# Scores of a cross attention from high and low parts in f32r, with the keys' low part made by the vector engine

## The chip, the cores and the metric

One core of one Trainium2 chip. The metric is the device time of one execution in microseconds. The kernel is one program that computes two decoder layers; the change is in its first stage.

## The reference, cut to what matters

The stage is the cross attention of layer 0. 8 sequences of 64 query tokens (512 wide, 16 heads of 32) look at a context of 1601 tokens of width 256. The last 16 tokens are handled apart; the main attention is over 1585 keys.

```python
q = _ln((x @ Wq + bq).reshape(b, s1, H, HD), qn_w, qn_b)
kv = jnp.concatenate([y_main @ Wk + bk, y_main @ Wv + bv], axis=-1)
kv = kv.reshape(b, s2, H, 2 * HD)
k = _ln(kv[..., :HD], kn_w, kn_b)
v = kv[..., HD:]
s = jnp.einsum('bhqd,bhkd->bhqk', q, k) * SCALE
p = jax.nn.softmax(s, axis=-1)
ctx = jnp.einsum('bhqk,bhkd->bhqd', p, v)
```

## The kernel before

`x0_main_attention` goes through the sequences one at a time, in two halves of 8 heads each. A half has 13 key tiles of 128 keys (the last has 49), so a sequence is 26 tile steps, numbered n = 0 to 25. All engines run the same list of steps, each its own part in a fixed order, tied by semaphores; between the first and the last sequence a hardware loop does two sequences a turn.

In step n:
- PE writes the scores of tile n, for 8 heads and 64 queries at once, into one of two PSUM banks (L828): two matmuls, g = 0 and 1, of 128 keys by 256 columns, with the keys `kT` as weights and `qbd` as moving operand. `qbd` holds the queries of four heads on a block diagonal, zero elsewhere, so that one matmul does four heads. PE waits for `kept` of tile n-2 first.
- DVE first subtracts the maximum from tile n-14 (L961), then scales tile n by the keys' inverse deviations while it moves it to the ring in SBUF (L983, `kept`), then takes the running maximum (L993).
- ACT does the exponential of tile n-14 (L1078), POOL adds it to the running sum (L889), and PE multiplies tile n-16 with the values (L854).
- At n = 14 and n = 1 a half's maximum is finished: PE transposes the running maximum (L838, one step earlier), DVE reduces it and rounds it (L1000, L1002, L1004), and PE spreads it (L799). `L799` stands ahead of all other work of PE in its step and waits for L1004.

Between these stand entries of four kinds, placed at steps by two strings: Y (transpose of the context), K (projection of keys), W (sums of squares of the keys, for the deviations) and V (projection of values). `HERE` are those for the sequence at hand, `AHEAD` those for the next:

```python
HERE = entries("0:K030 1:K031 2:W03 3:K100 4:K101 4:V0 5:W10 5:V1 6:K110 6:V2 7:K111 7:V3 8:W11 8:V4 9:K120 9:V5 "
               "10:K121 10:V6 11:W12 11:V7 12:V8 13:K130 13:V9 14:K131 14:Va 15:W13 15:Vb 16:Vc")
AHEAD = entries("12:Y00 13:Y01 15:Y10 16:Y11 16:K000 17:K001 18:W00 18:Y20 19:K010 20:K011 21:W01 21:Y21 "
                "22:K020 23:K021 24:W02 24:Y30 25:Y31")
```

Each entry uses one of three PSUM banks in turn. PE fills it, and another engine reads it and frees it. For Y, ACT writes the high part of the transposed context in f32r (L1034) and DVE the low part, what is left of the exact value (L111 by `split`). For K, ACT writes the keys with their bias to `kT` in f32 (L1040) and their squares to `sq` (L1042), and frees the bank. The projections Y feeds are already done with three f32r matmuls each, high by high, high by low and low by high (`matmul3`, L116 to L118).

DVE places the queries of the half after next in `qbd` at n = 0 and n = 13 (`place_queries`, four instructions of 32 rows, L913).

Of the kernel before, what the change touches and what calls it, by code (L numbers as in the profile page):

```python
# [14 lines left out]
F32 = mybir.dt.float32  # L15
F32R = mybir.dt.float32r
# [282 lines left out]
def half_at(part, n, step):  # L299

    for f in (-2, -1, 0, 1):
        if n == KT * f + step and not (f < 0 and part == "first"):
            return f
    return None
# [324 lines left out]
def x0_main_attention(nc, c, d, ps, qT, wkv, bk, kn, ctxT, y, load_context, y_loaded):  # L629
# [5 lines left out]
    with Stage(nc, "x0b") as st:  # L635
# [6 lines left out]
        kT = st.sb("kT", [P, 2, MAIN0])  # L642
# [3 lines left out]
        qbd = st.sb("qbd", [P, HG0, GC])  # L646
# [37 lines left out]
        for part, batches in (("prologue", [("before", -1), ("first", 0)]), ("body", [("body", 0), ("body", 1)]),  # L684
# [3 lines left out]
            for kind, rel in batches:  # L688
                for e in (BEFORE if kind == "before" else [(a, *e) for n in range(TILES) for a, e in made_at(kind, n)]):
# [7 lines left out]
                                                      st.sem("w_done"), st.sem("rstd_done"))  # L697
        v_done, q_placed = st.sem("v_done"), st.sem("q_placed")
# [24 lines left out]
        def place(at, e):  # L723
            part, i, rel = at
            return sched.find(part, i, (rel, *e))

        with nc.Block() as block:
# [9 lines left out]
            def _(pe):  # L737
# [54 lines left out]
                def step(part, at, seq, par, n):  # L792
# [25 lines left out]
                    if n < TILES:  # L818
# [8 lines left out]
                        for g in range(2):  # L827
                            mm = pe.matmul(ps[0:m, S_BANK + n % 2, g * GC:(g + 1) * GC], kT[:, g, kt * P:kt * P + m],  # L828
                                           qbd[:, 2 * half + g, :], start=True, stop=True)
# [67 lines left out]
            def _(v):  # L897
                v.memset(qbd[:, :, :], 0.0).then_inc(zeroed, 1)
# [3 lines left out]
                v.wait_ge(zeroed, 4)  # L902
                for j in range(4):
                    v.memset(headsum[32 * j:32 * j + 32, j:j + 1], 1.0).then_inc(zeroed, 1)
                v.wait_ge(zeroed, 8)
# [4 lines left out]
                def place_queries(seq, half):  # L910
                    for j in range(4):
                        rows = slice(32 * j, 32 * j + 32)
                        v.tensor_scalar(qbd[rows, 2 * half:2 * half + 2, S * j:S * j + S],  # L913
                                        qT[rows, 2 * half:2 * half + 2, bass.ds(seq * S, S)], kn[rows, 0:1], None, ALU.mult
                                        ).then_inc(q_placed, 1)

                def take(at, seq, e):
                    bank, nth = place(at, e)
                    if e[1] == "Y":
# [105 lines left out]
            def _(act):  # L1025
                def take(at, seq, e):
# [8 lines left out]
                    if e[1] == "K":  # L1035
# [4 lines left out]
                        act.activation(kT[:, g, k0:k0 + n], src[:, 0:n], ACT.Identity, bias=bias).then_inc(k_done, 1)  # L1040
                        act.wait_ge(w_made, 8 * seq + (4 * half + j + 1))
                        act.activation(sq[g][:, 0:n], src[:, 0:n], ACT.Square, bias=bias).then_inc(sq_done, 1)  # L1042
                        act.wait_ge(sq_done, 16 * seq + (8 * half + 2 * j + g + 1))
                        act.sem_inc(kv_free[bank], 1)
# [20 lines left out]

                def step(part, at, seq, par, n):
                    f = half_at(part, n, 29)
# [2045 lines left out]
```

## Time and profile before

| | us |
|---|---|
| median of 3 runs | 2758.72 (2758.25 to 2759.28) |
| the profiled execution, its own time | 2750.2 |
| its span in the profile | 2747.5 |
| PE busy in the span | 2434.7 (89%) |
| DVE busy | 1719.2 (63%) |
| ACT busy | 1155.4 (42%) |
| POOL busy | 1002.0 (36%) |

The span goes from the first to the last instruction of the profiled execution. Busy time of PE is that of matmul records, whose ends are modelled; weight loads are recorded apart (PEld). An f32 matmul appears as two records. "Granted clock" is TensorE's clock as a share of 2.4 GHz. The first cross attention's main part begins at about 103 us and ends at about 973 us.

### The profile page before, as it was taken

The numbers are of one execution on the slowest core, as the hardware profiler recorded it, in microseconds if no ns is written. First come the engines' busy times: TensorE is split into PE (matmuls) and PEld (weight loads), VectorE is DVE, ScalarE is ACT, GpSimd is POOL, SyncE is SP. The second block draws the span as 40 slices with busy tenths as digits, with TensorE's granted clock in tenths as the row PEclk, the third lists the DMA queues.
The fourth block names the chain that finished last, engine by engine and source line by source line (L and its number), as shares of the span: only waits on it lengthen the run. The fifth ranks groups of instructions, "written<-read, shape, count | busy, mean of one in ns | idle before, by whom it ended". The sixth has DMA issues, their size and how long they took to land. (4 is left out here: it accounts for less than half of the span.)

```text
span 2747.5 us, 40047 instructions
## 1 busy us (share of the span) xinstructions
PE 2434.7 (89%) x12756; PEld 2003.8 (73%) x12756; DVE 1719.2 (63%) x2728; ACT 1155.4 (42%) x2084; POOL 1002.0 (36%) x688
## 2 busy tenths in 40 slices
PE   4699999999999969998898899999999997788744
PEld 2588888888888748886676678888888876566632
DVE  3457766766767723333443278888788884666677
ACT  1344444443444313332221367666676662332211
POOL 3147667667667610000011035544555460110000
PEclk9699999999999979998899899999999999899957
DMA  3000000000000012210231200000000002110010
GB/s 103 1 25 25 25 1 25 25 1 25 19 7 1 1 64 69 68 61 17 68 86 37 83 25 25 16 18 17 26 25 16 10 1 76 52 41 31 12 62 16
DMA packets 104256, 89.51 MB, mean 33 GB/s; under 512 B 32752, under 2 KB 82432, under 8 KB 104080
## 3 DMA queue, kind: packets, MB, share of 16 engines
q1 hardware_dynamic: 103792, 87.28, 10.5%
q8 instruction: 96, 1.57, 0.2%
q14 instruction: 80, 0.66, 0.1%
q0 software_dynamic: 288, 0.00, 0.0%
HBM read 86.22 MB, written 1.05 MB: 32 GB/s over the span
## 5 line engine op out<-in xcount | busy, mean ns | idle before, releaser
L2184 POOL TENSOR_TENSOR xT<-xT,x1b_ring 128x512 f32<-128x512 f32 (+1 forms) x176 | 248.3, 1411 | 213.4 <-ACT x1b_ring L2314 206.7
L869 POOL TENSOR_TENSOR x0b_krstd<-x0b_krstd,minus_half 128x24 f32<-128x24 f32 x64 | 267.0, 4173 | 108.7 <-DVE x0b_krstd L933 87.9
L889 POOL TENSOR_TENSOR xT<-xT,x0b_ring 128x512 f32<-128x512 f32 (+1 forms) x176 | 243.8, 1385 | 142.4 <-ACT x0b_ring L1078 130.6
L983 DVE TENSOR_TENSOR x0b_ring<-x_ps,x0b_krstd 128x512 f32<-128x512 f32 (+1 forms) x208 | 143.0, 688 | 134.4 <-PE x_ps L828 132.2
L111 DVE TENSOR_TENSOR x1b_plo<-x1b_ring,x1b_phi 128x512 fp32r<-128x512 f32 (+1 forms) x208 | 222.2, 1068 | 6.6 <-issue 4.9
L854 PE MATMUL x_ps<-x0b_ring,x0b_vn 128*128 128x256 f32 (+1 forms) x832 | 217.5, 386 | 1.8 <-ACT x0b_ring L1078 1.6
L828 PE MATMUL x_ps<-x0b_qbd,x0b_kT 128*128 128x256 f32 (+1 forms) x832 | 217.6, 384 | 1.6 <-DVE x0b_ring L983 1.4
L1078 ACT ACTIVATE x0b_ring<-x0b_ring 128x512 f32<-128x512 f32 (+1 forms) x208 | 130.7, 630 | 207.7 <-DVE x0b_ring L961 197.3
L2329 ACT ACTIVATE x1b_ring<-x_ps,x1b_keymask 128x512 f32<-128x512 f32 (+1 forms) x208 | 143.1, 688 | 131.3 <-DVE xT L2256 126.0
L116 PE MATMUL x_ps<-x1b_qy,x1b_yT 128*128 128x512 f32 (+1 forms) x416 | 175.8, 423 | 4.3 <-ACT x1b_ring L2329 2.9
L828 PEld LDWEIGHTS x_ps<-x0b_qbd,x0b_kT 128*128 128x128 f32 (+1 forms) x832 | 149.9, 187 | 30.1 <-issue 6.4
L854 PEld LDWEIGHTS x_ps<-x0b_ring,x0b_vn 128*128 128x128 f32 (+1 forms) x832 | 153.4, 191 | 23.9 <-issue 2.7
L116 PE MATMUL x_ps<-x1b_phi,x1b_yv 128*128 128x512 f32 (+1 forms) x416 | 166.6, 400 | 1.5 <-ACT x1b_out_sb L2296 1.5
L2256 DVE SCALAR_TENSOR_TENSOR xT<-x_ps,x1b_keymask,xT 128x512 f32<-128x512 f32 (+1 forms) x176 | 131.2, 745 | 57.7 <-PE x_ps L118 56.8
L993 DVE TENSOR_TENSOR xT<-xT,x0b_ring 128x512 f32<-128x512 f32 (+1 forms) x176 | 153.5, 872 | 17.9
L117 PE MATMUL x_ps<-x1b_qy,x1b_yT 128*128 128x512 f32 (+1 forms) x416 | 164.4, 395 | 0.0
L118 PE MATMUL x_ps<-x1b_qy,x1b_yT 128*128 128x512 f32 (+1 forms) x416 | 164.4, 395 | 0.0
L118 PE MATMUL x_ps<-x1b_phi,x1b_yv 128*128 128x512 f32 (+1 forms) x416 | 163.9, 394 | 0.0
L117 PE MATMUL x_ps<-x1b_plo,x1b_yv 128*128 128x512 f32 (+1 forms) x416 | 163.2, 392 | 0.0
L2314 ACT ACTIVATE x1b_ring<-x1b_ring 128x512 f32<-128x512 f32 (+1 forms) x208 | 131.1, 630 | 64.0 <-DVE x1b_ring L2225 63.0
L961 DVE TENSOR_TENSOR x0b_ring<-x0b_ring,x_ps 128x512 f32<-128x512 f32 (+1 forms) x208 | 141.3, 683 | 24.7 <-PE x_ps L799 10.6
L2225 DVE TENSOR_TENSOR x1b_ring<-x1b_ring,x_ps 128x512 f32<-128x512 f32 (+1 forms) x208 | 140.6, 676 | 2.0 <-PE x_ps L2094 2.0
(575 smaller groups left out, 5844.5 us busy)
## 6 DMA issues: line engine op xcount, KB each, us to landing
x_y<-in_ctx_dram SPq DMA_DIRECT2D x8, 1536.0 KB
x_y<-in_ctx_dram SPq DMA_DIRECT2D x24, 512.0 KB, 3.8
a_wn<-in_L_attn_W_Q_dram SPq DMA_DIRECT2D x16, 256.0 KB, 3.1
a_wn<-in_L_attn_W_K_dram SPq DMA_DIRECT2D x16, 256.0 KB, 3.5
a_wn<-in_L_attn_W_V_dram SPq DMA_DIRECT2D x16, 256.0 KB, 4.1
a_won<-in_L_attn_W_O_dram SPq DMA_DIRECT2D x16, 256.0 KB, 2.9
x1a_wq<-in_L_xattn_Wq_dram SPq DMA_DIRECT2D x4, 1024.0 KB, 10.7
x1c_wo<-in_L_xattn_Wo_dram SPq DMA_DIRECT2D x8, 512.0 KB, 6.9
```

Source lines behind the costliest of these rows:

```text
L111: return v.tensor_tensor(lo, exact, hi.bitcast(F32), ALU.subtract)
L116: pe.matmul(out, lhs[0], rhs[0], start=start, stop=False, **kw)
L117: pe.matmul(out, lhs[0], rhs[1], start=False, stop=False, **kw)
L118: return pe.matmul(out, lhs[1], rhs[0], start=False, stop=stop, **kw)
L828: mm = pe.matmul(ps[0:m, S_BANK + n % 2, g * GC:(g + 1) * GC], kT[:, g, kt * P:kt * P + m], qbd[:, 2 * half + g, :], start=True, stop=True)
L854: mm = pe.matmul(ps[:, O_BANK, g * GC:(g + 1) * GC], vn[0:m, kt, half, g * P:(g + 1) * P], ring[0:m, key_slot(par, t, LIFE), g * GC:(g + 1 ...
L869: ins = g_.tensor_tensor(r, r, c.minus_half[:, 0:8].unsqueeze(1).broadcast_to([P, whole, 8]), ALU.pow)
L889: g_.tensor_tensor(total[half][0:m, :], old, src, ALU.add).then_inc(summed, 1)
L983: v.tensor_tensor(slot.rearrange("p (h s) -> p h s", s=S), ps[0:m, S_BANK + n % 2, :].rearrange("p (h s) -> p h s", s=S), spread(krstd[0:m ...
L993: v.tensor_tensor(run[half][0:m, :], before, slot, ALU.max).then_inc(max_done, 1)
L2184: g_.tensor_tensor(total[half][0:m, :], old, src, ALU.add).then_inc(summed, 1)
L2329: act.activation(ring[0:m, key_slot(par, n, LIFE), :], ps[0:m, S_BANK + n % 2, :], ACT.Identity, bias=keymask[0:m, kt:kt + 1]).then_inc(ke ...
```

## The change

`kT` and `qbd` become pairs of f32r tiles, a high and a low part. The scores are taken with `matmul3`. For each K entry ACT squares first, then writes the high part of the keys; DVE reads the same bank again, adds the bias, subtracts the high part and writes the low part, and then frees the bank. For the queries ACT writes the high part into the block diagonal and DVE the low part, each in four instructions of 32 rows. Both `qbd` tiles are zeroed at the start.

```diff
-        kT = st.sb("kT", [P, 2, MAIN0])
+        kT = [st.sb(f"kT{i}", [P, 2, MAIN0], F32R) for i in ("hi", "lo")]
-        qbd = st.sb("qbd", [P, HG0, GC])
+        qbd = [st.sb(f"qbd{i}", [P, HG0, GC], F32R) for i in ("hi", "lo")]
...
                         for g in range(2):
-                            mm = pe.matmul(ps[0:m, S_BANK + n % 2, g * GC:(g + 1) * GC], kT[:, g, kt * P:kt * P + m],
-                                           qbd[:, 2 * half + g, :], start=True, stop=True)
+                            mm = matmul3(pe, ps[0:m, S_BANK + n % 2, g * GC:(g + 1) * GC],
+                                         [a[:, g, kt * P:kt * P + m] for a in kT], [a[:, 2 * half + g, :] for a in qbd],
+                                         start=True, stop=True)
...
             def _(v):
-                v.memset(qbd[:, :, :], 0.0).then_inc(zeroed, 1)
+                for a in qbd:
+                    v.memset(a[:, :, :].bitcast(F32), 0.0).then_inc(zeroed, 1)
...
-                        v.tensor_scalar(qbd[rows, 2 * half:2 * half + 2, S * j:S * j + S],
-                                        qT[rows, 2 * half:2 * half + 2, bass.ds(seq * S, S)], kn[rows, 0:1], None, ALU.mult
-                                        ).then_inc(q_placed, 1)
+                        hi, lo = (a[rows, 2 * half:2 * half + 2, S * j:S * j + S] for a in qbd)
+                        v.wait_ge(q_hi, 8 * seq + (4 * half + j + 1))
+                        v.scalar_tensor_tensor(lo, qT[rows, 2 * half:2 * half + 2, bass.ds(seq * S, S)], kn[rows, 0:1],
+                                               hi.bitcast(F32), ALU.mult, ALU.subtract).then_inc(q_placed, 1)
...
+                    if e[1] == "K":
+                        _, _, half, j, g = e
+                        k0, n = keys_of(j)
+                        i = 16 * seq + (8 * half + 2 * j + g + 1)
+                        hi, lo = (a[:, g, k0:k0 + n] for a in kT)
+                        v.wait_ge(k_hi, i)
+                        v.scalar_tensor_tensor(lo, ps[:, bank, 0:n], kbias[:, 2 * half + g:2 * half + g + 1],
+                                               hi.bitcast(F32), ALU.add, ALU.subtract).then_inc(k_done, 1)
+                        v.wait_ge(k_done, i)
+                        v.sem_inc(kv_free[bank], 1)
...
                         act.wait_ge(kv_full[bank], nth + 1)
-                        act.activation(kT[:, g, k0:k0 + n], src[:, 0:n], ACT.Identity, bias=bias).then_inc(k_done, 1)
                         act.wait_ge(w_made, 8 * seq + (4 * half + j + 1))
                         act.activation(sq[g][:, 0:n], src[:, 0:n], ACT.Square, bias=bias).then_inc(sq_done, 1)
-                        act.wait_ge(sq_done, 16 * seq + (8 * half + 2 * j + g + 1))
-                        act.sem_inc(kv_free[bank], 1)
+                        act.activation(kT[0][:, g, k0:k0 + n], src[:, 0:n], ACT.Identity, bias=bias).then_inc(k_hi, 1)
...
+                def place_queries(seq, half):
+                    for j in range(4):
+                        rows = slice(32 * j, 32 * j + 32)
+                        act.activation(qbd[0][rows, 2 * half:2 * half + 2, S * j:S * j + S],
+                                       qT[rows, 2 * half:2 * half + 2, bass.ds(seq * S, S)], ACT.Copy, scale=kn[rows, 0:1]
+                                       ).then_inc(q_hi, 1)
+
+                act.wait_ge(zeroed, 9)
+                place_queries(0, 0)
+
                 def step(part, at, seq, par, n):
+                    if n == 0:
+                        if part != "first":
+                            act.wait_ge(scored, TILES * seq)
+                        place_queries(seq, 1)
+                    if n == KT and part != "last":
+                        act.wait_ge(scored, TILES * seq + KT)
+                        place_queries(seq + 1, 0)
```

## Rows read from the trace of the kernel before

**Rows 1.** Windows: span, busy us of each engine (instructions), granted clock, DMA share, GB/s.

```profile
185.00:972.00 787.00, 753.71 (x4026) 649.49 (x4025) 544.34 (x919) 340.34 (x601) 523.61 (x264) 0.99 0.04 13
497.21:544.57 47.36, 45.90 (x256) 39.73 (x257) 37.01 (x64) 21.90 (x41) 33.69 (x17) 1.00 0.06 16
544.57:599.26 54.69, 54.12 (x288) 47.08 (x289) 34.96 (x58) 23.71 (x41) 35.24 (x18) 1.00 0.05 17
```

**Rows 2.** Waits, 199 to 972 us: who for whom, us, times, longest.

```profile
DVE x0b_ring L983 <- PE x_ps L828: 111.5, 88, 3.1
...
DVE x0b_yT L111 <- ACT x0b_yT L1034: 37.4, 29, 2.7
...
PE x_ps L799 <- DVE x0b_rowmax L1004: 20.9, 13, 5.4
```

**Rows 3.** Timeline of PE, two places: start, us, line, operation, count.

```profile
207.58 0.34 PE L117 MATMUL x_ps<-x0b_yT,x_wkv 128*128 128x384 f32 x1
...
208.28 0.34 PE L118 MATMUL x_ps<-x0b_yT,x_wkv 128*128 128x384 f32 x1
...
519.33 1.03 PE L828 MATMUL x_ps<-x0b_qbd,x0b_kT 128*128 128x256 f32 x4
...
522.11 1.03 PE L828 MATMUL x_ps<-x0b_qbd,x0b_kT 128*128 128x256 f32 x4
```

**Rows 4.** One line's instructions: duration in ns, least, median, most.

```profile
L828 PE MATMUL x_ps<-x0b_qbd,x0b_kT x832: 377/379/634, 141.0 to 940.4; 128*128 128x256 f32 x154, 128*49 128x256 f32 x13
```

**Rows 5.** Timeline of PE in a later stage, f32 of 128 columns.

```profile
1022.57 3.74 PE L1274 MATMUL a_ps<-a_wvT,xT 128*128 128x128 f32 x32
```

**Rows 6.** Timeline of DVE in the light stretch.

```profile
513.76 0.69 DVE L961 TENSOR_TENSOR x0b_ring<-x0b_ring,x_ps 128x512 f32<-128x512 f32 x1 [0.15 <-DVE x0b_yT L111]
...
523.36 0.68 DVE L961 TENSOR_TENSOR x0b_ring<-x0b_ring,x_ps 128x512 f32<-128x512 f32 x1
...
525.37 0.68 DVE L961 TENSOR_TENSOR x0b_ring<-x0b_ring,x_ps 128x512 f32<-128x512 f32 x1
...
528.36 0.69 DVE L111 TENSOR_TENSOR x0b_yT<-x_ps,x0b_yT 128x512 fp32r<-128x512 f32 x1 [0.80 <-ACT x0b_yT L1034]
...
532.24 0.69 DVE L983 TENSOR_TENSOR x0b_ring<-x_ps,x0b_krstd 128x512 f32<-128x512 f32 x1 [0.33 <-PE x_ps L828]
...
535.02 0.69 DVE L983 TENSOR_TENSOR x0b_ring<-x_ps,x0b_krstd 128x512 f32<-128x512 f32 x1 [0.68 <-PE x_ps L828]
...
537.91 0.21 DVE L111 TENSOR_TENSOR x0b_yT<-x_ps,x0b_yT 128x49 fp32r<-128x49 f32 x1 [0.24 <-DVE x0b_krstd L933]
...
540.82 1.21 DVE L913 TENSOR_SCALAR x0b_qbd<-x_qT,x_kn 32x128 f32 x4 [0.34 <-PE x_ps L828]
...
544.28 0.16 DVE L1004 TENSOR_TENSOR x0b_rowmax<-x0b_rowmax,x0b_qshift 128x4 f32<-128x4 f32 x1
```

**Rows 7.** Timeline of PE: three of L799, with the idle time before.

```profile
440.08 1.11 PE L799 MATMUL x_ps<-ident,x0b_rowmax 128*128 128x128 f32 x4 [5.21 <-DVE x0b_rowmax L1004]
...
497.21 0.65 PE L799 MATMUL x_ps<-ident,x0b_rowmax 128*128 128x128 f32 x4 [0.21 <-DVE x0b_rowmax L1004]
...
544.57 0.65 PE L799 MATMUL x_ps<-ident,x0b_rowmax 128*128 128x128 f32 x4 [1.46 <-DVE x0b_rowmax L1004]
```

**Rows 8.** Timeline of ACT in one step of the same stretch.

```profile
524.07 0.63 ACT L1078 ACTIVATE x0b_ring<-x0b_ring 128x512 f32<-128x512 f32 x1 [0.44 <-DVE x0b_ring L961]
524.61 0.57 ACT L1040 ACTIVATE x0b_kT<-x_ps,x0b_kbias 128x384 f32<-128x384 f32 x1
525.07 0.57 ACT L1042 ACTIVATE x0b_sq<-x_ps,x0b_kbias 128x384 f32<-128x384 f32 x1
```

**Rows 9.** A scalar_tensor_tensor from PSUM in a later stage, duration in ns.

```profile
L2256 DVE SCALAR_TENSOR_TENSOR xT<-x_ps,x1b_keymask,xT x176: 733/747/753, 1585.8 to 2238.2; 128x512 f32<-128x512 f32 x160, 65x512 f32<-65x512 f32 x16
```

**Rows 10.** Timeline at the start of the main part.

```profile
103.33 0.91 DVE L898 MEMSET x0b_qbd<- 128x1024 f32 x1 [5.15 <-PEq L383]
```

**Rows 11.** Windows, behind the wait at 440.08.

```profile
440.00:444.00 4.00, 3.92 (x12) 3.47 (x13) 1.71 (x3) 0.63 (x1) 0.00 (x0) 0.50 0.00 0
```

More of the change, by code:

```diff
@@ L697, in x0_main_attention @@
                                                       st.sem("w_done"), st.sem("rstd_done"))
+        k_hi, q_hi = st.sem("k_hi"), st.sem("q_hi")
         v_done, q_placed = st.sem("v_done"), st.sem("q_placed")
@@ L901, in _ @@
                     v.memset(a[:, :, MAIN0:MAIN0 + 1].bitcast(F32), 0.0).then_inc(zeroed, 1)
-                v.wait_ge(zeroed, 4)
+                v.wait_ge(zeroed, 5)
                 for j in range(4):
                     v.memset(headsum[32 * j:32 * j + 32, j:j + 1], 1.0).then_inc(zeroed, 1)
-                v.wait_ge(zeroed, 8)
+                v.wait_ge(zeroed, 9)
                 v.tensor_scalar(headkn[:, :], headsum[:, :], kn[:, 1:2], None, ALU.mult).then_inc(ready, 1)
```

## The prediction

> **What bounds the kernel now.** I read the windows first. The first cross attention's main part runs from 185 to 972 us. There TensorE (PE) is busy 753.7 of 787.0 us at full clock, VectorE (DVE) 544.3, ScalarE (ACT) 340.3 and GpSimd (POOL) 523.6 [rows 1]. So PE sets the pace on average. But the same view, cut at the places where PE stands still (below), shows two unlike halves of one batch. From tile step 1 to 14 (54.69 us) DVE is busy 35.0 us. From step 14 to step 1 of the next batch (47.36 us) it is busy 37.0 us [rows 1]. The schedule strings explain it: value projections stand only at steps 4 to 16, so PE's long steps are there, and steps 17 to 25 hold little more than scores, probabilities-times-values and a key projection.
>
> The waits say the same from the other side [rows 2]. DVE stands 111.5 us for the scores of PE, which is slack. PE stands 20.9 us for the row maxima of L1004, which is the place where DVE sets the end: L799 at steps 14 and 1 waits for it, and all later PE work is behind L799. So a batch is two stretches, each ended by that wait. I call 1 to 14 the heavy stretch and 14 to 1 the light one.
>
> **Price of the scores.** A 256-column f32 matmul is two records. Four records of L828 span 1.03 us and one record lasts 379 ns, so records start (1.03-0.38)/3 = 0.217 us apart, 0.868 us a tile [rows 3, 4]. The new form issues six f32r matmuls of 256 columns a tile. The trace has none of that size. Its nearest is 384 columns: five starts over 0.70 us, 0.175 apart, which is 0.160 of streaming (384 columns at 2.4 GHz, the granted clock being 1.00) and 0.015 more [rows 1, 3]. At 256 columns that makes 0.107+0.015 = 0.122, and a tile 0.732 us. I take this. Lower bound: pure streaming, 0.107, a tile 0.64. Upper bound: a weight load that no longer hides; 32 records of a 128x128 load with 0.107 us of streaming in f32 take 3.74 us, at most 0.117 each [rows 5], so loads do keep up at that pace, and the bound from far off is the 0.175 of the 384-column form, a tile 1.05 us.
>
> The Trainium skill ("TensorE: Matmul & The Clock Gate", Part 3, The mechanism) speaks against the change: it says a weight load overlaps a running matmul only when the row groups differ. With its load of columns/1.2 ns a record would be about 0.107+0.107 us, and the tile 1.28 us against 0.87, an estimate of +86 us over 208 tiles. The 384-column records, 0.175 apart with a 128-column load in each, do not agree with it; by it they would be 0.27 apart.
>
> So PE is relieved of 0.868-0.732 = 0.136 us a tile, 28.3 us over 208 tiles (bounds: 47 us less, 38 us more). What arrives at the end depends on who paces.
>
> **Heavy stretch, PE paces.** DVE has some 20 us of idle time there [rows 1] and takes its share of the new work within it: half a batch's 16 K entries, at most 8 x 0.8 = 6 us. Steps 1 to 13 give 13 x 0.136 = 1.77 us. The wait at step 14 was 0.21 us [rows 7]; its chain (score of tile 12, placing of queries, tile 13, row maximum) does not shorten with the score of tile 13 and gets about 0.1 us longer, since the first ACT copy must precede DVE's first subtraction. I take 1.5 us a batch, 8 batches: -12 us.
>
> **Light stretch, DVE paces.** From its subtraction at step 17 (513.76) to the end of the row maximum (544.28 + 0.16) DVE works 30.7 us, and its waits for others are only 0.80 (L111), 0.33 and 0.68 (L983) and 0.34 (L913): 2.15 us [rows 6]. Its bare step is 25.37-23.36 = 2.01 us. PE's step with a key projection is 522.11-519.33 = 2.78 us, 2.64 after the change [rows 3].
> - New DVE instruction: one scalar_tensor_tensor from PSUM for each of 16 K entries a batch. At 128x512 that operation takes 0.747 us [rows 9]; the tensor_tensor L111 takes 0.69 at 512 and 0.21 at 49 elements, so 1.04 ns an element [rows 6]. For 384 elements: 0.61 us (bounds 0.56 in proportion, 0.75 as it stands). Behind it DVE waits for its own write before it frees the bank, 0.15 us as after L111 [rows 6]: 0.76 us.
> - New wait: DVE now stands for ACT's high part, as it did for L111. ACT's order is exponential, square, high part. In a saturated step DVE's subtraction starts at 523.36, ACT's exponential at 524.07, its two K operations at 524.61 and 525.07, and the second ends 525.64 [rows 8], 2.28 us after the subtraction. DVE is free after 2.01. So each handover costs about 0.27 us even with PE ahead. The step is 2.28+0.76 = 3.04 us, more than PE's 2.64: PE then runs at most two tiles ahead (it waits for `kept` of tile n-2) and stands still. Behind DVE's wait stand the next subtraction and so ACT's next exponential; the K bank is freed later too, but with three banks its next user comes two steps later.
> - Six K entries lie in the saturated part (steps 16, 17, 19, 20, 22, 23). Six instructions: 4.56 us. Four handovers (at 16 and 17 ACT is early): 1.08. Together 5.64. The idle 2.15 us vanishes into them. Placing adds 0.1. PE reaches step 17 earlier by 3 x 0.136 = 0.4. Net 5.64-2.15+0.1-0.4 = +3.2 us for each of the seven light stretches that hold a next batch: +22 us. If no handover cost anything it would be +2.1 each, +15; if each of the six took 0.75+0.15 and waited 0.3, +4.7, +33. The last batch has no K entries there: nothing.
>
> **The rest.** Eight 32-row query copies a batch go to ACT, which is idle over half the time [rows 1], each shorter than the 0.46 us between two K operations [rows 8], while DVE still finishes its last split. Without that cover 16 times four of them would be at most 29 us. The first placing is not covered: four copies stand ahead of ACT's first output, and a second memset of 0.91 us [rows 10] ahead of the first matmul, together +2.5 us. Squares now come first, so the four W entries before batch 0 start one ACT operation earlier, 4 x 0.46 = 1.8 less. Net +1 (bounds -1 to +3). The keys' high part costs ACT what the plain copy cost. No DMA changes.
>
> **Sum.** -12+22+1 = +11 us. The profiled execution took 2750.2 us (span 2747.5) and the median of the runs is 2758.7, 8.5 more, so 2761 in the profile and **2770 us** in the median.
>
> **Rivals.**
> 1. *PE paces everywhere (the other side).* The 111.5 us for which DVE waits [rows 2] hides all its new work, and all 28.3 us arrive: 2758.7-28.3+1 = 2731 us. It decides where a light K step of DVE stays under PE's 2.64 us, against the 3.04 worked out. Against it: that slack is in the heavy stretch. With the 0.107 records it would reach 2713. Chance 0.18.
> 2. *The handover is as long as L111's.* There DVE waited 37.4 us for ACT in 29 waits, 1.3 us each, or 0.8 over the 48 large ones of 8 batches [rows 2]. Six waits of 0.8 a stretch instead of 1.08 in all: +3.7x7 = 26, 2796 us. Against it: the long ones are at Y entries whose transposes come last in PE's step. Chance 0.13.
> 3. *Loads show at 256 columns.* A record takes 0.145, nothing is gained on PE: +12 heavy, +3 light, 2785 us. By the skill's rule above it would be far worse. Chance 0.07.
> 4. *The clock.* At 440.08 PE stood 5.21 us, and over the next 4 us the granted clock was 0.50, that is 1.2 GHz [rows 7, 11]; after the 1.46 us at 544.57 it stayed 1.00. The following heavy stretch is 57.1 against 54.7 us. If the longer stand at step 1 does this in five more light stretches: up to 5 x 2.4, taken as +9, 2779 us. The skill's same page (HAM oscillation) also warns of it. For it: PE's stand before L838 and L799 grows by over 3 us. Against it: part is spread over the scores. Chance 0.15.
>
> **Numbers.** The forecast has chance 0.47, and its own range is 2758 to 2784. From 2738 to 2798 about half of rival 1 and half of rival 2 fall outside, 0.15 in all. Measurement tells 0.2%, 5.5 us. Faster is rival 1 and a sliver of the main case, 0.20; within 0.2% is the low tail of the main case, 0.12; slower is the rest, 0.68.
>
> **What would show it.** Records of L116 to L118 with kT and qbd 0.12 us apart (under 0.11 or over 0.14 is wrong). Heavy stretches (L799 to L799) near 53 us, light ones near 50.5 or more with PE idle before L828, L838 and L799. New DVE instructions near 0.61 us, their waits for ACT about 0.3 in the light stretch. DVE waits for L828 nearly gone from steps 17 to 25. The prediction is wrong if light stretches get shorter, which means DVE was not the pacer; or if heavy ones grow, which means banks held longer stop PE, a cost put at nothing here.

## The result and the profile after

The changed kernel takes 2791.01 us (median of 4 runs, 2789.17 to 2794.21), the kernel before 2758.48 beside it (4 runs). The ratio is 1.0135, with a 95% interval of 1.0116 to 1.0155: slower by 33 us by the medians and by 37 by the ratio, where +11 was forecast. I call it 35 below. The profiled execution of the changed kernel took 2789.17 us and its span is 2787.4, against 2747.5 before. One execution each of e6_low_later and e14_spread_no_low below fell in a slower state of the chip and is left out of their times and run counts.

Lines have moved: old L799 is L800 (its last operand from DVE, old L1004, is now L1018), L838 is L840, L828 is now L116 to L118, L961 is L975, L983 is L997, L993 is L1007. L929 is the new instruction for the keys' low part, L932 frees its bank, L918 is the queries' low part, L1055 ACT's square, L1056 its high part of the keys, L1081 that of the queries, L770 PE's sums of squares. L1107 is ACT's exponential, L856 PE's product with the values; L1014 and L1016 are the first two instructions of the row maximum (old L1000 and L1002); L1023 and L1030 add a finished half to the context.

I cut both traces at L799/L800 into seven pairs of stretches and added them up:

| stretches | before | after | difference | forecast |
|---|---|---|---|---|
| seven light ones (step 14 to step 1) | 337.6 | 371.6 | +34.0, 4.9 each | +3.2 each |
| seven heavy ones (step 1 to step 14) | 384.6 | 392.5 | +7.9, 1.1 each | -1.5 each |

So both halves missed to the same side. All else together is 2 us shorter. Windows of the changed kernel: us, busy us of PE, PEld, DVE, ACT and POOL (instructions), granted clock, DMA share, GB/s. The rows of before are [rows 1].

```profile
185.00:980.00 795.00, 729.32 (x4317) 653.61 (x4316) 608.95 (x999) 343.27 (x635) 505.72 (x248) 0.95 0.04 13
566.12:622.32 56.20, 53.53 (x314) 48.01 (x314) 43.11 (x67) 24.89 (x46) 34.09 (x17) 0.97 0.03 9
512.79:566.12 53.33, 47.36 (x283) 42.73 (x283) 41.59 (x73) 22.93 (x44) 35.62 (x17) 0.94 0.08 23
346.00:348.00 2.00, 2.00 (x7) 1.77 (x7) 1.16 (x2) 0.73 (x2) 0.00 (x0) 0.50 0.00 0
540.00:544.00 4.00, 1.44 (x13) 1.24 (x11) 3.54 (x5) 1.72 (x4) 3.75 (x3) 0.97 0.00 0
544.00:548.00 4.00, 4.00 (x16) 3.64 (x16) 3.35 (x7) 1.14 (x2) 2.92 (x3) 0.50 0.00 0
566.00:570.00 4.00, 3.88 (x26) 3.68 (x27) 2.74 (x5) 1.77 (x3) 0.00 (x0) 1.00 0.38 121
582.00:586.00 4.00, 2.01 (x9) 1.59 (x9) 3.59 (x7) 0.63 (x1) 1.18 (x1) 0.84 0.00 0
586.00:590.00 4.00, 4.00 (x19) 3.52 (x18) 2.08 (x4) 1.23 (x2) 3.97 (x2) 0.73 0.00 0
```

The third row is a light stretch (before 47.36 us), the second the heavy one behind it (before 54.69). In the light one PE is idle for 6 us where it was idle for 1.5. The granted clock of the whole part fell from 0.99 to 0.95, and the small windows show where: it is 0.50 (1.2 GHz) right behind one stand of PE (540 to 544), and the 0.84 and 0.73 around another are means of both levels. Behind the stand at step 1 it stays 1.00 in this batch (566 to 570), but not in every one: two batches earlier (346 to 348) it is 0.50. Of the seven heavy stretches four lose the full clock behind step 1 and four behind step 5.

What PE waited for, 199 to 1010 us, and two of DVE's waits (us, times, longest):

```profile
DVE x0b_kTlo L929 <- ACT x0b_kThi L1056: 41.7, 63, 1.9
DVE x0b_ring L997 <- PE x_ps L118: 34.3, 54, 2.6
PE x_ps L800 <- DVE x0b_rowmax L1018: 29.5, 14, 5.4
...
PE x_ps L770 <- ACT x0b_sq L1055: 16.1, 8, 2.6
...
PE x_ps L116 <- DVEq L932: 12.1, 7, 2.0
...
PE x_ps L840 <- DVE xT L1007: 6.0, 6, 2.8
```

DVE's slack against PE's scores went from 111.5 to 34.3 us [rows 2]. PE's wait for the row maximum grew from 20.9 to 29.5, and two waits are large that were not in [rows 2]: for the squares (L770) and for a bank that DVE has not freed (L932). PE around these places:

```profile
344.38 0.65 PE L800 MATMUL x_ps<-ident,x0b_rowmax 128*128 128x128 f32 x4 [2.82 <-DVE x0b_rowmax L1018]
...
539.88 0.27 PE L117 MATMUL x_ps<-x0b_qbdlo,x0b_kThi 128*128 128x256 f32 x1
540.00 0.28 PE L118 MATMUL x_ps<-x0b_qbdhi,x0b_kTlo 128*128 128x256 f32 x1
542.83 1.88 PE L770 MATMUL x_ps<-x0b_headsum,x0b_sq 128*128 128x4 f32 x12 [2.56 <-ACT x0b_sq L1055]
...
545.46 1.91 PE L856 MATMUL x_ps<-x0b_ring,x0b_vn 128*128 128x256 f32 x4
...
566.12 0.65 PE L800 MATMUL x_ps<-ident,x0b_rowmax 128*128 128x128 f32 x4 [2.83 <-DVE x0b_rowmax L1018]
...
576.51 0.28 PE L118 MATMUL x_ps<-x0b_qbdhi,x0b_kTlo 128*128 128x256 f32 x1
576.63 0.28 PE L116 MATMUL x_ps<-x0b_qbdhi,x0b_kThi 128*128 128x256 f32 x1
576.76 0.27 PE L117 MATMUL x_ps<-x0b_qbdlo,x0b_kThi 128*128 128x256 f32 x1
...
581.00 1.40 PE L770 MATMUL x_ps<-x0b_headsum,x0b_sq 128*128 128x4 f32 x12
584.39 0.50 PE L116 MATMUL x_ps<-x_wkv,x0b_yT 128*128 128x512 f32 x1 [1.99 <-DVEq L932]
```

The score records start 0.12 us apart (539.88 to 540.00, 576.51 to 576.63), as forecast. DVE at the same places:

```profile
537.86 0.69 DVE L975 TENSOR_TENSOR x0b_ring<-x0b_ring,x_ps 128x512 f32<-128x512 f32 x1 [0.15 <-DVE x0b_yT L111]
...
540.19 0.62 DVE L929 SCALAR_TENSOR_TENSOR x0b_kTlo<-x_ps,x0b_kbias,x0b_kThi 128x384 fp32r<-128x384 f32 x1 [0.22 <-ACT x0b_kThi L1056]
540.96 0.69 DVE L975 TENSOR_TENSOR x0b_ring<-x0b_ring,x_ps 128x512 f32<-128x512 f32 x1 [0.15 <-DVE x0b_kTlo L929]
...
551.78 0.62 DVE L929 SCALAR_TENSOR_TENSOR x0b_kTlo<-x_ps,x0b_kbias,x0b_kThi 128x384 fp32r<-128x384 f32 x1 [1.58 <-ACT x0b_kThi L1056]
...
561.05 1.47 DVE L918 SCALAR_TENSOR_TENSOR x0b_qbdlo<-x_qT,x_kn,x0b_qbdhi 32x128 fp32r<-32x128 f32 x4 [0.41 <-ACT x0b_qbdhi L1081]
...
564.58 1.21 DVE L1016 TENSOR_TENSOR x0b_rowmax<-x0b_rowmax,x0b_qshift 128x4 f32<-128x4 f32 x1
...
580.40 0.67 DVE L1023 TENSOR_TENSOR x0b_osb<-x0b_osb,x_ps 128x512 f32<-128x512 f32 x1
581.21 2.42 DVE L1030 TENSOR_TENSOR x_ctxT<-x0b_osb,x_ctxT 32x128 f32 x4
583.66 0.62 DVE L929 SCALAR_TENSOR_TENSOR x0b_kTlo<-x_ps,x0b_kbias,x0b_kThi 128x384 fp32r<-128x384 f32 x1
```

And ACT before the stand at 540:

```profile
541.68 0.63 ACT L1107 ACTIVATE x0b_ring<-x0b_ring 128x512 f32<-128x512 f32 x1 [1.53 <-DVE x0b_ring L975]
542.22 0.56 ACT L1055 ACTIVATE x0b_sq<-x_ps,x0b_kbias 128x384 f32<-128x384 f32 x1
```

Three readings.
- **Step 21 (540 us).** DVE's step with a K entry is 3.10 us (L975 at 537.86 and 540.96; forecast 3.04). DVE falls behind PE, its subtraction comes late, ACT's exponential waits for it, ACT's square stands behind the exponential, and PE's sums of squares (W01) wait for the square: 2.56 us. The same stand of 2.56 us is there in the six light stretches from 291 on. The forecast had only the scores, L838 and L799 in mind as the places where DVE's lateness reaches PE.
- **Step 5 (584 us).** DVE's low part of a K entry stands behind the accumulation of the finished half: one L1023 and four L1030, 3.2 us from 580.40. The bank is held as long, and PE's next projection into it (V1) stands 1.99 us. Seven batches show this, with 1.25 to 2.00 us.
- **Step 1 (566 us).** The stand is 2.83 us where it was 1.46 [rows 7]. It is not the K entry that grew here: the queries' low parts take 1.47 instead of 1.21 us [rows 6] and L1016 takes 1.21 us, where the trace of before has 0.16 for it (old L1002) in the same place. Over all seven stands at step 1 the growth is smaller, 18.6 to 24.0 us, 0.8 each: it is 1.4 in three batches and not there at the turns of the hardware loop, where PE stood over 5 us already.

The traces also show what goes with a long L1016. Rows of before, DVE and POOL, and of the changed kernel, POOL:

```profile
544.08 0.16 DVE L1002 TENSOR_TENSOR x0b_rowmax<-x0b_rowmax,x0b_qshift 128x4 f32<-128x4 f32 x1
...
544.34 1.26 POOL L889 TENSOR_TENSOR xT<-xT,x0b_ring 49x512 f32<-49x512 f32 x1 [0.27 <-POOL xT L889]
...
564.51 1.25 POOL L891 TENSOR_TENSOR xT<-xT,x0b_ring 49x512 f32<-49x512 f32 x1 [0.27 <-POOL xT L891]
```

In the changed kernel POOL's instruction starts at 564.51, ahead of L1016 (564.58), and L1016 ends at 565.79, 0.03 us behind it. Before, POOL's starts at 544.34, when L1002 is done. All 14 long L1016 of the changed kernel and all 11 long L1002 of before have an instruction of POOL running at their start and end 0.02 to 0.04 us behind its end. No run moves POOL's work alone, so this is read and not tested.

The new instruction's price is as forecast. Groups by line and shape, 199 to 1010 us (busy us, mean ns of one, and the idle time before):

```profile
L929 DVE SCALAR_TENSOR_TENSOR x0b_kTlo<-x_ps,x0b_kbias,x0b_kThi 128x384 fp32r<-128x384 f32 x84 | 51.7, 616 | 29.2 <-ACT x0b_kThi L1056 28.4
...
L929 DVE SCALAR_TENSOR_TENSOR x0b_kTlo<-x_ps,x0b_kbias,x0b_kThi 128x433 fp32r<-128x433 f32 x28 | 18.7, 669 | 13.4 <-ACT x0b_kThi L1056 13.4
```

### The profile page after: what moved, and what is told of

The parts are those of the page before. It is cut to its first block and busy times, and to the rows that moved or that the text cites. A ratio compares the mean times of both kernels' runs of the same rounds, so it can differ in the third digit from the quotient of the medians.

```text
span 2787.4 us, 41223 instructions
## 1 busy us (share of the span) xinstructions
PE 2428.8 (87%) x13172; PEld 2023.7 (73%) x13172; DVE 1814.9 (65%) x2857; ACT 1172.7 (42%) x2148; POOL 1005.9 (36%) x688
## 3 DMA queue, kind: packets, MB, share of 16 engines
HBM read 86.22 MB, written 1.05 MB: 31 GB/s over the span
## 5 line engine op out<-in xcount | busy, mean ns | idle before, releaser
L1107 ACT ACTIVATE x0b_ring<-x0b_ring 128x512 f32<-128x512 f32 (+1 forms) x208 | 130.9, 631 | 309.9 <-DVE x0b_ring L975 308.7
L856 PE MATMUL x_ps<-x0b_ring,x0b_vn 128*128 128x256 f32 (+1 forms) x832 | 227.2, 399 | 1.9 <-ACT x0b_ring L1107 1.6
L116 PE MATMUL x_ps<-x1b_qy,x1b_yT 128*128 128x512 f32 (+1 forms) x416 | 176.0, 423 | 4.3 <-ACT x1b_ring L2358 2.9
L856 PEld LDWEIGHTS x_ps<-x0b_ring,x0b_vn 128*128 128x128 f32 (+1 forms) x832 | 159.6, 199 | 25.9 <-issue 3.2
L1007 DVE TENSOR_TENSOR xT<-xT,x0b_ring 128x512 f32<-128x512 f32 (+1 forms) x176 | 159.5, 906 | 19.0 <-DVE x0b_ring L997 1.5
L997 DVE TENSOR_TENSOR x0b_ring<-x_ps,x0b_krstd 128x512 f32<-128x512 f32 (+1 forms) x208 | 142.7, 686 | 44.0 <-PE x_ps L118 41.7
L116 PE MATMUL x_ps<-x1b_phi,x1b_yv 128*128 128x512 f32 (+1 forms) x416 | 166.3, 400 | 1.5 <-ACT x1b_out_sb L2325 1.5
L975 DVE TENSOR_TENSOR x0b_ring<-x0b_ring,x_ps 128x512 f32<-128x512 f32 (+1 forms) x208 | 142.0, 686 | 35.2 <-DVE x0b_kTlo L929 17.2
L118 PE MATMUL x_ps<-x1b_qy,x1b_yT 128*128 128x512 f32 (+1 forms) x416 | 164.3, 395 | 0.0
L118 PE MATMUL x_ps<-x1b_phi,x1b_yv 128*128 128x512 f32 (+1 forms) x416 | 164.1, 395 | 0.0
L116 PE MATMUL x_ps<-x0b_qbdhi,x0b_kThi 128*128 128x256 f32 (+1 forms) x416 | 152.2, 366 | 4.0 <-DVE x0b_ring L997 3.8
L111 POOL TENSOR_TENSOR x1b_yv<-x_y,x1b_yv 128x256 fp32r<-128x256 f32 (+1 forms) x104 | 87.2, 838 | 144.1 <-ACT x1b_yv L2372 142.8
```

What stands on the lines that cost most here:

```text
L111: return v.tensor_tensor(lo, exact, hi.bitcast(F32), ALU.subtract)
L116: pe.matmul(out, lhs[0], rhs[0], start=start, stop=False, **kw)
L118: return pe.matmul(out, lhs[1], rhs[0], start=False, stop=stop, **kw)
L856: mm = pe.matmul(ps[:, O_BANK, g * GC:(g + 1) * GC], vn[0:m, kt, half, g * P:(g + 1) * P], ring[0:m, key_slot(par, t, LIFE), g * GC:(g + 1 ...
L975: v.tensor_tensor(slot, slot, ps[0:m, M_BANK, :], ALU.subtract).then_inc(shifted, 1)
L997: v.tensor_tensor(slot.rearrange("p (h s) -> p h s", s=S), ps[0:m, S_BANK + n % 2, :].rearrange("p (h s) -> p h s", s=S), spread(krstd[0:m ...
```

## The experiments

My theory after the result: DVE's K work costs far more than its own time in stretches that it paces, because it also delays what others take from DVE in the heavy half. The rivals: the longer hold of the bank or the handover alone; the loss of the clock alone; PE's new score records giving nothing. All ratios are to the kernel before, run beside; one per cent is about 27.5 us. Sums are over the seven light and the seven heavy stretches of the profiled execution. That is one run and can lie off the median: by 10 us in e5 and 13 in e10, most of it behind this stage, by 8 (below) in the kernel before, by under 5 in the others.

**e1_no_low.** The low part of the keys is never made (POOL zeroes that tile once, and PE waits for it at the start); ACT frees the bank. The third matmul of each score still runs.

```diff
-                        v.wait_ge(k_hi, i)
-                        v.scalar_tensor_tensor(lo, ps[:, bank, 0:n], kbias[:, 2 * half + g:2 * half + g + 1],
-                                               hi.bitcast(F32), ALU.add, ALU.subtract).then_inc(k_done, 1)
-                        v.wait_ge(k_done, i)
-                        v.sem_inc(kv_free[bank], 1)
+                        pass
...
+                        act.wait_ge(k_done, 16 * seq + (8 * half + 2 * j + g + 1))
+                        act.sem_inc(kv_free[bank], 1)
```

> Leaves out the low part of the keys (that tile stays zero, so the third f32r matmul of each score adds nothing but still runs); ACT frees the K bank itself behind its two reads, as before the change. Theory A, the vector engine's new K instruction with its handover is the whole loss: the relief of PE arrives in full. Six records of 256 columns lie 0.118 us apart in the trace after, 0.71 us a tile instead of 0.868, so 208 x 0.158 = 33 us less than before and about 3 us more at the start: near 2729 us. Theory B, something else of the change loses the time (queries placed by two engines, the added waits of ACT): at or above 2758 us, and the light stretches stay over 50 us. Between them: each share as the time says.

Measured: 2735.97 us (4 runs), ratio 0.9933 [0.9918, 0.9947]. Light 336.6, heavy 374.7. Against the changed kernel that is 0.0202, some 56 us: the whole price of the K work on DVE. And without it the new scores gain only 18 us, not 28: the light stretches are as long as before (336.6 to 337.6). One part of that is the stand at step 1, which is 2.85 us here too and 5.9 us longer than before over the seven batches; the rest is not split up.

```profile
537.92 0.65 PE L802 MATMUL x_ps<-ident,x0b_rowmax 128*128 128x128 f32 x4 [2.85 <-DVE x0b_rowmax L1018]
```

Its DVE shows the same chain as the changed kernel's, queries' low parts and a long L1016, with no K work of DVE near.

```profile
533.34 1.10 DVE L922 SCALAR_TENSOR_TENSOR x0b_qbdlo<-x_qT,x_kn,x0b_qbdhi 32x128 fp32r<-32x128 f32 x3 [0.15 <-issue]
...
536.50 1.10 DVE L1016 TENSOR_TENSOR x0b_rowmax<-x0b_rowmax,x0b_qshift 128x4 f32<-128x4 f32 x1
```

**e2_hold_only.** DVE waits for ACT's high part and frees the bank, but makes no low part.

```diff
-                        v.scalar_tensor_tensor(lo, ps[:, bank, 0:n], kbias[:, 2 * half + g:2 * half + g + 1],
-                                               hi.bitcast(F32), ALU.add, ALU.subtract).then_inc(k_done, 1)
-                        v.wait_ge(k_done, i)
+                        v.sem_inc(k_done, 1)
```

> Leaves out the low part of the keys (that tile stays zero), but the vector engine still waits for ACT's high part in its place, and still is the one that frees the bank. If the instruction's own time on the vector engine (16 x 0.77 us a batch) is what costs: close to the kernel without any of it, within 8 us of 2729. If the handover and the bank held by the vector engine's late turn are what costs: close to the changed kernel, 2775 to 2790, with TensorE still standing 2 us for the bank at step 5 of each batch and for the squares at step 21.

Measured: 2747.33 us (10 runs), ratio 0.998 [0.9967, 0.9994]. Light 345.0, heavy 377.5. So the wait for ACT and the longer hold cost 0.0047 (13 us), and the instruction itself, with its own wait behind it, 0.0155 (43 us): from e2 to the changed kernel the light stretches grow by 26.6, 3.8 each, the heavy ones by 15.0, 2.1 each. The stand at step 5 is not there in e2: the bank's place in DVE's order alone does not make it. A heavy stretch of e2 has the same granted clock as that of the changed kernel, 0.97, with the half clock behind step 1; so what the low part costs there is mostly the stand at step 5 itself and not the clock behind it.

```profile
230.44:284.50 54.06, 53.38 (x315) 48.04 (x315) 35.10 (x58) 25.03 (x45) 34.28 (x17) 0.97 0.02 6
```

**e3_f32_scores.** All is made as in the changed kernel, but the score is one f32 matmul of the two high parts.

```diff
-                            mm = matmul3(pe, ps[0:m, S_BANK + n % 2, g * GC:(g + 1) * GC],
-                                         [a[:, g, kt * P:kt * P + m] for a in kT], [a[:, 2 * half + g, :] for a in qbd],
-                                         start=True, stop=True)
+                            mm = pe.matmul(ps[0:m, S_BANK + n % 2, g * GC:(g + 1) * GC],
+                                           kT[0][:, g, kt * P:kt * P + m].bitcast(F32),
+                                           qbd[0][:, 2 * half + g, :].bitcast(F32), start=True, stop=True)
```

> All of the change's work on ACT and DVE is kept, but the scores are again one f32 matmul each, of the high parts alone (the low parts are written and not read). It tells what f32r scores are worth once the vector engine has its new work. If DVE sets the pace in the light stretches and PE in the heavy ones: about half of 33 us is lost, 2791 + 12 to 20 = 2803 to 2811. If PE sets the pace everywhere: 2824. If DVE does everywhere: 2791 to 2795.

Measured: 2806.89 us (4 runs), ratio 1.019 [1.0175, 1.0205]. Light 367.6, heavy 408.8. The faster scores are worth 0.0055, 15 us, beside this DVE work; all of it is in the heavy stretches (408.8 to 392.5), and none in the light ones, which are 4 us longer with the faster scores (367.6 to 371.6). This is the plainest sign that DVE paces the light stretches.

**e6_low_later.** DVE takes a K entry one step later, behind that step's subtraction, so that ACT's high part is there already.

```diff
+                    while late:
+                        take(*late.pop(0))
...
-                        take(at, seq + ahead, (ahead, *e))
+                        if e[0] == "K":
+                            late.append((at, seq + ahead, (ahead, *e)))
+                        else:
+                            take(at, seq + ahead, (ahead, *e))
```

> Only the place of the vector engine's K work changes: it is taken one step later, behind that step's first subtraction. The subtraction then no longer waits for ACT's high part, and ACT's exponential and squares are released earlier; the bank is held some 0.8 us longer. If the handover loop (subtraction, exponential, square, high part, low part) and the squares that come late for PE are a large part of the loss: a light K step falls from 3.1 to about 2.8 us, the 2.6 us wait of PE for squares at step 21 shrinks, and the time falls to 2770 to 2780. If the bank held longer is what costs: 2795 or more, with PE's wait for a bank at step 5 longer than 2.0 us. If it is the instruction's time alone: 2788 to 2792.

Measured: 2804.62 us (5 runs), ratio 1.0186 [1.0172, 1.0199]. Light 387.0, heavy 393.7: 14 us worse than the change as it was made, all of it in the light stretches. PE's waits:

```profile
PE x_ps L116 <- DVEq L932: 19.3, 13, 1.8
...
PE x_ps L770 <- ACT x0b_sq L1061: 9.4, 7, 1.5
PE x_ps L116 <- DVE x0b_yT L111: 8.4, 6, 2.1
```

Sparing DVE its wait for ACT and holding the bank a step longer trades one for the other: the squares come earlier (16.1 to 9.4 us), but the stands for a bank go from 7 to 13 (12.1 to 19.3 us), and waits for the transposed context grow from 1.2 to 8.4. The wait for ACT was not the costly part, as e2 says too.

**e8_fill.** The changed kernel with work that PE does for nothing while it stands: 14 transposes of the identity before V1's wait for its bank (step 5), 20 before W01's wait for the squares (step 21).

```diff
+                def fill(read, count):
+                    pe.wait_ge(normed, read)
+                    for _ in range(count):
+                        pe.transpose(ps[:, X_BANK, 0:P], c.ident[:, :], c.ident[:, :])
+
...
+                    if e[1:] == ("V", 1):
+                        fill(2 * seq + 1, 14)
                     pe.wait_ge(kv_free[bank], nth + 1)
+                    if e[1:] == ("W", 0, 1) and at != ("prologue", 0, -1):
+                        fill(2 * seq, 20)
```

> The changed kernel with PE kept busy in two of its new stands: 14 transposes of the identity (0.11 us each) into an unused bank ahead of the wait for a bank at step 5, and 20 ahead of the wait for squares at step 21. The result is unchanged. If the half clock that follows those stands is a good part of the loss (granted clock 0.94 in light and 0.97 in heavy stretches against 1.00), PE keeps 2.4 GHz there, the light stretches fall by 1 us or more and the heavy ones by 1: 2770 to 2780. If the clock only slows PE where it waits for DVE anyway, nothing changes or it gets slower by what the transposes overrun: 2789 to 2800.

Measured: 2780.92 us (6 runs), ratio 1.0089 [1.0071, 1.0106]. Light 364.3, heavy 389.7. The granted clock from 199 to 900 us is 0.98, against 0.95 in the changed kernel and 0.99 before. PE is as late as it was, but busy:

```profile
539.27 2.35 PE L742 MATMUL x_ps<-ident 128*128 128x128 f32 x20
...
541.99 1.50 PE L779 MATMUL x_ps<-x0b_headsum,x0b_sq 128*128 128x4 f32 x12 [0.37 <-ACT x0b_sq L1064]
```

So about 13 us (0.0046) of the loss is time at half clock behind these stands. The rest, 0.0089, is there at nearly full clock: light stretches still 26.7 us over those of before, heavy ones 5.1. The half clock is not all gone: with the other two stands filled it lies behind the stand at step 1 in each of the seven heavy stretches. In the batch at 564:

```profile
565.00:569.00 4.00, 4.00 (x16) 3.50 (x15) 2.04 (x4) 1.77 (x3) 0.00 (x0) 0.57 0.02 6
```

**e4_spread, e5_spread_before, e14_spread_no_low.** The same strings of entries in three kernels: the changed one, the one before, and e1. Value projections are moved out of steps 5 to 15 until six of the 13 stand at steps 16 to 22 (one before), where PE had slack and DVE had none; three of the Y entries stand two steps later.

```diff
-        HERE = entries("0:K030 1:K031 2:W03 3:K100 4:K101 4:V0 5:W10 5:V1 6:K110 6:V2 7:K111 7:V3 8:W11 8:V4 9:K120 9:V5 "
-                       "10:K121 10:V6 11:W12 11:V7 12:V8 13:K130 13:V9 14:K131 14:Va 15:W13 15:Vb 16:Vc")
-        AHEAD = entries("12:Y00 13:Y01 15:Y10 16:Y11 16:K000 17:K001 18:W00 18:Y20 19:K010 20:K011 21:W01 21:Y21 "
+        HERE = entries("0:K030 1:K031 2:W03 3:K100 4:K101 4:V0 5:W10 6:K110 6:V1 7:K111 8:W11 8:V2 9:K120 10:K121 10:V3 "
+                       "11:W12 12:V4 13:K130 13:V5 14:K131 14:V6 15:W13 16:V7 17:V8 18:V9 19:Va 19:Vb 22:Vc")
+        AHEAD = entries("12:Y00 13:Y01 16:K000 17:Y10 17:K001 18:W00 18:Y11 19:K010 20:Y20 20:K011 21:W01 21:Y21 "
```

> The changed kernel with the schedule strings changed: the 13 value projections stand at steps 4 to 22 instead of 4 to 16, and the context transposes Y10, Y11 and Y20 two steps later, since the projections read the tiles that they overwrite. The same instructions in all. If DVE sets the pace in the light stretches and PE in the heavy ones, then moving PE work from the one to the other makes both engines' loads lie over each other: PE's total is about 96 us a batch less than 1 us of waits, and the loss falls to half or less, 2760 to 2775 us, with light stretches longer and heavy ones shorter by more. If the loss sits in chains that go with the K entries wherever PE's work lies (the bank held, squares late): 2788 or more.

> The kernel before with the same changed schedule strings, as a control. PE sets its pace in nearly all steps, so only its stands of 0.2 and 1.5 us a batch are there to win: within 8 us of 2754 to 2758. If it becomes faster by as much as the changed kernel does, the schedule is better as such and says nothing on the change.

> The spread schedule, and the keys' low part left out as in e1_no_low (the low tile stays zero, ACT frees the bank). It prices the vector engine's K work under a schedule in which PE's work is even. If the price comes from DVE lying alone in the light stretches, it is small here: under 20 us between this and e4_spread, against 55 us between e1_no_low and the changed kernel: 2732 to 2745. If the price is one of the instructions wherever they lie, it is as large, and this kernel comes out near 2700.

| kernel | us (runs) | ratio | light | heavy |
|---|---|---|---|---|
| e4, with the change | 2750.42 (12) | 0.9983 [0.9971, 0.9994] | 376.9 | 346.5 |
| e5, on the kernel before | 2759.34 (12) | 1.0023 [1.0005, 1.004] | 380.6 | 347.2 |
| e14, on e1 | 2741.53 (5) | 0.9943 [0.9924, 0.9961] | 375.7 | 342.0 |

With V entries spread out, the change with all its DVE work beats the kernel before, by 0.17%, and beats the change as it was made by 40 us. The spread by itself is no gain (e5), so under the new strings the change gains 0.0040, some 11 us (e4 less e5). And the K work on DVE, 56 us under the old strings (changed kernel less e1), costs 0.0040, 11 us (5 to 17 by the two intervals), under the new ones (e4 less e14). The same instructions: their price is one of place. In e4 PE's waits for a bank and for squares are nearly gone,

```profile
PE x_ps L800 <- DVE x0b_rowmax L1018: 31.5, 14, 3.3
...
PE x_ps L770 <- ACT x0b_sq L1055: 4.5, 7, 0.7
...
PE x_ps L116 <- DVEq L932: 1.5, 5, 0.3
```

and a heavy stretch of it has the full clock and DVE busy for 40.76 us of a stretch that is 7 us shorter:

```profile
549.56:599.00 49.44, 46.76 (x291) 42.44 (x291) 40.76 (x67) 22.02 (x42) 34.98 (x17) 1.00 0.02 7
```

**e12_place_after, e11_place_before, e10_spread_place, e13_spread_place6.** The placing of queries moved from steps 0 and 13, where it stands in the chain of the row maximum, to steps 6 and 16, on DVE and, where it has a part, on ACT; e13 moves only the one of step 0.

```diff
-                    if n == 0:
+                    if n == 6:
...
-                    if n == KT and part != "last":
+                    if n == KT + 3 and part != "last":
```

> The changed kernel, its schedule strings as they are, with the placing of queries moved to steps 6 and 16. If the queries made by two engines in turn are a part of the loss, the stand at step 1 falls from 2.8 to about 1.5 us and that at step 14 vanishes: 2765 to 2780. If the keys' part alone is the loss, the gain equals that of e11, 8 to 14 us: 2777 to 2783.

> The kernel before with its placing of queries moved to steps 6 and 16 (DVE alone, four instructions, 1.2 us). Control for e10_spread_place: its stands there are 1.5 and 0.2 to 0.6 us, so at most 8 x 2 = 16 us to win, likely 8 to 14: 2742 to 2750. The difference to e12 tells how much of the change's loss lies in the queries' part of it.

> The changed kernel with the spread schedule of e4_spread, and both halves of the placing of queries (ACT's and DVE's) moved from steps 0 and 13 to steps 6 and 16, away from the row maximum's chain. In the changed kernel PE stands 2.8 us at step 1 and 1.6 at step 14 for that chain; the placing and its handover take some 1.9 us of it. If that chain sets the end there, each stand shrinks by 1 to 1.9 us: 8 x 2 to 8 x 3 = 16 to 24 us less than 2750, 2726 to 2734. If DVE's total work sets the pace instead, moving it changes nothing: 2745 to 2755.

> The spread schedule of e4_spread, with only the placing at step 0 moved, to step 6; the other stays at step 13. In e10_spread_place the placing at step 16 fell into the steps before 21 and PE stood 2.6 us for squares in each batch, which ate the gain. Without that, the stand at step 1 shrinks from 2.8 to about 1.1 us and no new one comes: 8 x 1.7 = 14 us less than e4_spread, near 2737, ratio about 0.993. If the stand only moves to another place again: 2748 to 2753, ratio near 0.998, and the vector engine's chain is the bound throughout.

| kernel | us (runs) | ratio | light | heavy | stand at step 1, batch at 550 |
|---|---|---|---|---|---|
| e12, changed | 2772.3 (7) | 1.0065 [1.0042, 1.0088] | 358.7 | 385.0 | 1.10 |
| e11, before | 2748.26 (12) | 0.9975 [0.9955, 0.9995] | 332.0 | 387.1 | 1.30 |
| e10, e4 | 2752.31 (13) | 0.9994 [0.998, 1.0009] | 367.8 | 363.1 | 1.10 |
| e13, e4, step 0 only | 2765.57 (11) | 1.0036 [1.0021, 1.005] | 365.2 | 372.0 | 1.11 |

The move takes 19 us (0.0070) from the changed kernel and 7 us (0.0025) from the one before, so some 12 us of the loss (2 to 22 by the intervals) go with the placing at that place. About 6 of them are not the queries' own: over the seven batches L1016 takes 4.2 us less in e12 than in the changed kernel, and L1002 1.5 us more in e11 than before, as POOL's instruction does or does not run over it. The two gains do not add up: on top of e4 the move gives nothing or costs, though the stand at step 1 shrinks. What is gained there is lost at the squares, here in e10:

```profile
PE x_ps L770 <- ACT x0b_sq L1055: 18.4, 7, 2.7
```

and in e13, where the placing at step 13 stayed, so that moving it is not what makes these stands:

```profile
PE x_ps L770 <- ACT x0b_sq L1055: 17.9, 7, 2.7
```

The granted clock of e10 from 199 to 900 us is 0.96, where e4 has 0.99. I take it that PE, let go earlier at step 1, meets a DVE that is no further on, which no run shows; and why e13 is slower than e10 stays open.

## Why the prediction failed, and where it held

- **PE's price held.** Records of scores start 0.12 us apart (0.122 forecast, within the bounds of 0.107 and 0.175). Rival 3 is out. By the rule of the Trainium skill ("TensorE: Matmul & The Clock Gate", Part 3, The mechanism), that a weight load overlaps a running matmul only when the row groups differ, they would be about 0.21 apart, an estimate; the trace does not agree. The section excepts loads into a background weight buffer, and no row here shows whether these are such.
- **The price of DVE's instruction held.** 0.616 us for 384 elements (0.61), 0.15 us behind it, a step of 3.10 (3.04). The wait for ACT is 0.22 at 540.19 (0.27), but 3.1 us over the light stretch where 1.08 was forecast. Rival 2 is out as a price of its own: e2 prices waits and holding at 13 us for all stretches, where it said 26.
- **The light stretch had the right pacer and was undersized,** +4.9 against +3.2. e3 confirms the pacer (faster scores give nothing there), e1 that the gain of 0.4 at its head does not arrive. Terms of its sum that were off, in the stretch from 512.79: "PE reaches step 17 earlier by 0.4" (DVE's subtraction there is at 16.7 us, where it was at 16.6); "the idle 2.15 us vanishes into them" (2.7 us of waits for others are there, 1.58 of them at 551.78 for a high part, behind PE's stand and half clock); and "placing adds 0.1" (0.3, and L1016 1.05 more for meeting POOL). The forecast followed DVE's lateness to the scores, L838 and L799, not through ACT's exponential to the squares and PE's stand of 2.56 us at step 21, with its half clock.
- **The step that failed is the heavy stretch:** "PE paces ... and takes its share of the new work within it", -1.5 a batch, with "banks held longer stop PE" put at nothing. It is +1.1. The 20 us that DVE is idle there [rows 1] are an average over the stretch. Right behind step 1 DVE is behind, and at step 4 L1023 and L1030 add 3.2 us ahead of a K entry; PE stands up to 2 us for the bank. e2 shows that PE's gain would have been there (377.5, against 384.6 before), and that the low part's own time takes it away: 15.0 us over seven stretches. From -1.5 to +1.1 is 7 x 2.6 = 18 us, and the light stretches' 1.7 each are 12: together the 28 us by which the profiled executions missed the forecast, to within 2.
- **Rival 4, the clock, was true in part** and is not an alternative but a term: 13 us by e8 for steps 21 and 5, forecast +9 for step 1. Its place was half right: the stand at step 1 did grow, and behind it the clock fell to 0.50 in four of the seven batches (at 346, not at 566), two of them at loop turns, as before; with the other stands filled (e8) it fell in all seven. The larger part lies behind stands of 2.56 us at step 21, which the forecast did not have. The same page of the Trainium skill (HAM oscillation) warns of a clock that falls when PE waits between groups of matmuls; the trace agrees at 544 us and at 346, and not at 566.
- **Rival 1 is out for this schedule.** Even without any K work on DVE (e1) only 18 of the 28 us arrive, and the light stretches gain 1 us in all. What paces them then was not tried; the stand at step 1 is a part.
- **DVE's waits for scores** were to be nearly gone from steps 17 to 25; they fell from 111.5 to 34.3 us over all. The forecast gave longer heavy stretches as a sign of being wrong, and that sign came.
- **What was right** is the direction, and the pacer of the light half. The error is in the heavy half first and in size in the light one.

## What to carry to other kernels

The idle time of an engine over a stretch hides new work only if it lies behind the instructions that others wait for; walk the engine's order step by step, and for each new instruction name the longest thing queued ahead of it (here 3.2 us of accumulation ahead of a bank's release). An engine that falls behind reaches the bottleneck by every chain that starts on it, not only by the one that was last before. And after moving work from one engine to another, move the schedule's other work too: the same change costs 35 us or gains some 11, each against a kernel with the same strings, by where the value projections stand.

## What the runs showed of the hardware

- A 128x128 weight load is hidden behind an f32r matmul of only 256 columns: starts 0.12 us apart, where 256 columns at the granted 2.4 GHz are 0.107.
- A stand of PE of 2.56 us was followed by a granted clock of 0.50, one of 1.99 by 0.84 and 0.73 over two stretches of 4 us, one of 2.82 at step 1 (344.38) by 0.50, but one of 2.83 there (566.12) by 1.00. What tells them apart the runs do not say. Filling two of the stands moved the half clock to a third place.
- The same DVE instruction on 128x4 elements (L1016) takes 161 ns at least, 780 in the median and 1236 at most, and each of the 14 long ones ends 0.02 to 0.04 us behind an instruction of POOL that was running when it started. In the view of one line:

```profile
L1016 DVE TENSOR_TENSOR x0b_rowmax<-x0b_rowmax,x0b_qshift x16: 161/780/1236, 187.1 to 986.9; 128x4 f32<-128x4 f32 x16
```
